# A two-layer gated block on one core: when the token combinations of the first feed-forward pass are made

## The reference, cut to what matters

```
x = x + tanh(g_xattn[0]) * linear_attention(layernorm(x), ctx, ctx)
x = x + tanh(g_ffn[0])   * ffn0(layernorm(x))        # weights stored as 4-bit codes
x = x + tanh(g_xattn[1]) * autocorrelation(layernorm(x), ctx, ctx)
x = x + tanh(g_ffn[1])   * ffn1(layernorm(x))

ffn0(x1):
    Wg, Wu, Wd = NF4[codes] * absmax per block of 64         # 1024 -> 2752 -> 1024
    y1 = x1 @ Wg + x1 @ g_lora_a @ g_lora_b
    y2 = x1 @ Wu + x1 @ u_lora_a @ u_lora_b
    x3 = relu(y1) * y2
    return x3 @ Wd + x3 @ d_lora_a @ d_lora_b
```

## Time and profile before

| | us |
|---|---|
| median of 3 runs | 2003.04 (2002.95 to 2003.74) |
| the profiled execution | 2003.48 |
| its span, first to last instruction | 2001.5 |
| first matmul of pass 0's products (start) | 187.65 |
| first matmul of pass 1 (start) | 346.25 |

### The profile page before, as it was taken

The page is one execution under the profiler, slowest core; times in us unless marked ns, Lnnn a source line. Parts: engine busy times, 40 slices in busy tenths (PEclk is TensorE's granted clock), DMA queues, the critical chain, the costliest instruction groups (busy, mean ns, idle before and its releaser), DMA issues. The chain is left out here.

```text
span 2001.5 us, 26467 instructions
## 1 busy us (share of the span) xinstructions
PE 1918.8 (96%) x9140; PEld 963.6 (48%) x9140; DVE 1293.8 (65%) x2204; ACT 1254.9 (63%) x1998; POOL 835.4 (42%) x752
## 2 busy tenths in 40 slices
PE   6996888999999999999999999999998899999998
PEld 5774334444444444444444445444444455555554
DVE  5776888364564736555473644636379988888872
ACT  6995668886777677676777776677524343443431
POOL 2443884222223223232232333222268667667742
PEclk9997998999999999999999999999999999999999
DMA  5651545856637375573737556373531110111001
GB/s 201 223 171 55 193 163 195 292 193 215 232 122 265 105 257 190 178 249 127 265 109 252 192 172 227 99 253 117 210 137 59 32 41 29 53 53 38 27 22 42
DMA packets 91989, 303.01 MB, mean 151 GB/s; under 512 B 11984, under 2 KB 16720, under 8 KB 73168
## 3 DMA queue, kind: packets, MB, share of 16 engines
q1 hardware_dynamic: 91856, 301.32, 44.3%
HBM read 274.01 MB, written 27.26 MB: 151 GB/s over the span
## 5 line engine op out<-in xcount | busy, mean ns | idle before, releaser
L1036 ACT ACTIVATE first<-first 128x512 f32<-128x512 int32 x1008 | 625.7, 626 | 27.4 <-DVE wt L1439 1.8
L1265 POOL TENSOR_TENSOR gu<-wt,gu 128x512 f16<-128x512 f32 x86 | 102.3, 1190 | 370.6 <-ACT gu L1055 370.5
L1439 DVE SCALAR_TENSOR_TENSOR wt<-first,w_scale,absm 128x512 f32<-128x512 f32 x132 | 102.6, 777 | 227.4 <-ACT first L1036 226.8
L1785 PE MATMUL a_psQ<-z,gu 128*128 128x512 f16 x936 | 208.5, 379 | 0.0
L2386 PE MATMUL a_psL<-z,l_x 128*128 128x512 f16 x768 | 170.7, 379 | 1.0 <-DVE l_x L2488 0.8
L1785 PE MATMUL a_psC<-z,gu 128*128 128x512 f16 x732 | 167.8, 379 | 0.0
L1785 PE MATMUL a_psC<-z 128*128 128x512 f16 x684 | 156.9, 379 | 0.0
L1785 PEld LDWEIGHTS a_psQ<-z,gu 128*128 128x128 f16 x936 | 91.5, 98 | 110.5
L1277 POOL TENSOR_TENSOR hid_lo<-z,hid_hi 128x512 f16<-128x512 f32 x76 | 90.2, 1201 | 118.7 <-ACT hid_hi L1096 118.6
L1265 POOL TENSOR_TENSOR dn_lo<-wt,dn_hi 128x512 f16<-128x512 f32 x42 | 50.3, 1197 | 199.2 <-ACT dn_hi L1055 199.2
L1442 DVE SCALAR_TENSOR_TENSOR wt<-a_psE,lora_gain,wt 128x512 f32<-128x512 f32 x132 | 99.1, 751 | 44.6 <-PE a_psE L1747 24.4
(11 more groups left out here) (418 smaller groups left out, 4122.3 us busy)
## 6 DMA issues: line engine op xcount, KB each, us to landing
z<-x_parts SPq DMA_DIRECT2D x140, 1024.0 KB, 5.8
first<-in_codes SPq DMA_DIRECT2D x132, 256.0 KB, 3.0
absm<-in_absmax SPq DMA_DIRECT2D x264, 128.0 KB, 3.3
X<-in_x SPq DMA_DIRECT2D x16, 512.0 KB, 4.3
c_in<-in_ctx SPq DMA_DIRECT2D x16, 512.0 KB, 5.3
cT<-in_ctxT SPq DMA_DIRECT2D x16, 512.0 KB, 3.6
o_sp<-in_w SPq DMA_DIRECT2D x16, 512.0 KB, 4.8
z<-in_ctx SPq DMA_DIRECT2D x8, 1024.0 KB, 7.0
```

The lines of the kernel that those rows point to most:

```text
L1036: act.activation(level[w % 2][:], codes[w % RING] if k == 0 else level[w % 2][:], ACT.Prelu, bias=bias, scale=scale, alpha=alpha).then_inc ...
L1265: pool.tensor_tensor(low, source, high, ALU.subtract).then_inc(wlo_done, 1)
L1439: dve.scalar_tensor_tensor(wt[at], source[:], w_scale[:, m:m + 1], absm[w % RING][:], ALU.mult, ALU.mult).then_inc(scaled, 1)
L1785: mm = pe.matmul(out, w[:, k * P:(k + 1) * P], xx[:, k], start=first and q == 0, stop=q == 3 * KD // 2 - 1, skip_group_check=True)
```

## The change

Two edits. `folding` spreads the sixteen parts otherwise: in the product steps they stand in steps 1, 2, 4, 5, 7, 8, 10, 11, 13 and 14, two of three, and the last six stand in steps 16 to 21, beside the downs. The last three slots of the ring are filled in step 22 instead of 20.

```diff
         def folding(s):


-            i, part = divmod(s - 1, 2)
-            return (i, part) if 0 <= i < B else None
+            order = [t for t in range(1, 16) if t % 3] + list(range(16, 22))
+            return divmod(order.index(s), 2) if s in order else None
...
                         for t in range(2):
                             load_x(t)
-                    if s == 20:
+                    if s == 22:
                         for c in range(2):
                             sp.wait_ge(prod_mm[c], 8)
                         wait_parts(4 * B)
```

## The result

The changed kernel takes 2019.84 us (median of 4 runs, 2018.89 to 2020.17). The kernel before, run beside it, takes 2003.39; the ratio is 1.0078, 95% interval 1.0061 to 1.0096. The forecast of 2007.3 had the sign right and the size wrong: 12.5 us too low, and outside its range. The profiled execution is 2020.17 with a span of 2018.2, 16.7 us longer than before.

What follows compares the result with a forecast made beforehand. PE, busy 96% of the span, was taken as the bound; 10.4 us gained ahead of pair 7 and 14.3 lost behind it, taken as +4.3, made 2003.48 into 2007.8, median 2007.3, range 1998.8 to 2012.

Steps and rivals of the forecast that it cites:

- the product steps: Pass 0 ahead of the downs: DVE's hidden values of pair 7 start at 293.5 instead of 303.87, 10.4 us earlier.
- Unit 7: PE's 6.9 us wait in pass 0 for POOL's low half of weight unit 7, forecast to fall to about 4.
- the 5 us before the downs: PE's wait for DVE's hidden values of pair 7: of 8.2 us some 5 remain.
- the wait for `lora_b`: PE's 3.0 us wait on DVE in pass 0, forecast to shrink to about 1.
- DVE is the later one beside the downs: In the down steps, 21 combination instructions ahead of accumulate 20 make DVE late: 14.3 us lost behind pair 7.
- the sum: DVE's durations from pair 7's hidden values to the last combination, 47.7 us; with the product steps, +4.3 in all.
- S: PE's first matmul of pass 1, at 346.25 before, forecast at 350.2; its shift is carried to the end one for one.
- The clock rival: Close waits in the downs keep PE at 1.2 GHz, the six last downs take 7.8 us more: 2015; chance 0.05.
- pair 7 to S: From the start of DVE's hidden values of pair 7 to S: 56.7 us instead of 42.4.
- the forecast's own sign: If right, DVE has no wait of over 2 us from pair 7's hidden values to S.
- The ring: Slots 2 to 4 issued at 351.0 instead of 329.55; slot 2, needed at 360.8, comes in time: costed at nothing.
- Behind S: In pass 1 the first product copies are done by S + 9.8, PE wants them at S + 10.6: no loss.

Runs made afterwards that it cites:

- e4_both: Changed kernel with ring slots 0 and 1 filled in step 15 and the second layer's factor loads moved ahead of slots 3 and 4; ratio 1.0026.
- e7: As e4_both, but DVE's combination instructions of sequences 5 to 7 work on 16 of 512 columns; ratio 0.9981.
- e3: Changed kernel with ring slots 0 and 1 filled in step 15 instead of 18; ratio 1.0068.
- e2: Changed kernel with the loads of the second layer's two factors moved to step 22, ahead of ring slots 3 and 4; ratio 1.0045.
- e1: Kernel before with only the ring's edit, slots 2 to 4 in step 22; 2007.97 us against 2004.79, ratio 1.0013.
- e8: As e4_both, but POOL's combination instructions of sequences 5 to 7 work on 16 of 512 columns; ratio 0.9970.
- e12: Kernel before with steps 3, 7, 11, 15 free of combinations, five parts beside the downs, slots 0-1 in step 15, 2-4 in step 21; 2013.6 us, ratio 1.0041.
- e5: Kernel before with step 14 free of combinations, two parts in steps 16 and 17, ring unchanged; 1999.12 us, ratio 0.9972.
- e6: Kernel before with steps 14 and 16 free of combinations, parts in 17 and 18, slots 0 and 1 in step 15; 1999.52 us, ratio 0.9971.
- e9: Kernel before with steps 3, 9, 14 free of combinations, four parts beside the downs, slots 0-1 in step 15, 2-4 in step 21; 2013.1 us, ratio 1.0047.
- e10: Kernel before with steps 3, 7, 10, 14 free of combinations, five parts beside the downs, slots 0-1 in step 15, 2-4 in step 21; 2006.8 us, ratio 1.0012.

## Why the prediction was wrong

**Right: the product steps.** Pair 0 to pair 7 is 82.1 (forecast 293.5 - 211.85 = 81.7). Unit 7 and the 5 us before the downs came as walked, and the wait for `lora_b`, forecast at 1, is gone.

**Right in kind: DVE is the later one beside the downs.** e4_both, which leaves this and little else, is at 1.0026: 5.2 us where the sum had 4.3. In both kernels the 21 combination instructions took 21.7 us (forecast 22.9; mean 1.03 instead of 1.09), and from the last of them to S are 8.95 us (forecast 9.0). The closeness is partly luck: in e4_both DVE's waits are 3.7 us more than summed, and the other terms 2.4 less. The clock rival did not come about in the changed kernel: the granted clock, down to 0.50 in 325 to 330, is 1.00 in the last downs.

**Mis-sized: the waits inside pair 7 to S.** The last combination ends 52.1 us behind pair 7, forecast 47.7. DVE waits for POOL's low halves 1.88, 2.15 and 1.40 us, where the sum had 1.7 for them, and 3.55 for ACT's decoding of unit 16, where it had 0.5. By the forecast's own sign (no wait of DVE of over 2 us) both 2.15 and 3.55 spoke against it. The first error is of size: the chain through POOL and ACT is longer than walked, and e7, with DVE's share almost empty, still takes 49.6. The second is a step that was not there: the sum gave SP's stores their usual landing and did not ask what stood ahead of them on the queue. e3, and e4 with it, take 2.9 us of that wait away and shorten pair 7 to S by 2.4 and 3.0.

**Failed: "The ring" and "Behind S".** The ring was costed at nothing because its own slots would come in time, which they did: PE did not wait at its third product (364.04). I looked at what the ring's loads need and who needs them, and not at what stands behind them on the same queue. "Behind S: No loss" compared the copies with PE's need by ACT's work alone; L1134, which stands between the copies of the first and the second product, waits for a transfer. It cost 7.8 us (28.97 - 21.16), and e2 shows it by taking it away whole. Put at nothing, this is the largest part of the miss. The profiled execution lies 12.4 us above the sum: 7.8 here, 4.3 in pair 7 to S (61.0 instead of 56.7), 1.7 in the second layer (below), and -1.4 for the rest, mostly an earlier start of pair 0. The row was to be had before: ACT already waited 2.44 us there, with 1.9 to spare for PE.

The Trainium skill (DMA: Bandwidth & Descriptors, Queues, rings and completion order) says that each DMA engine takes the descriptors of one queue's ring in ring order. By this a small load waits until the large ones ahead of it have been served, and the rows agree: 11.7 instead of 6.4 us behind three slots, 9.5 instead of about 3 behind two. How much a load loses is not set by the slots ahead of it alone: behind one slot the later factor takes 7.8 us in e2 and 9.1 in e4_both, and what makes this difference is not shown.

**The last piece, 1.7 us.** It is far from the change, in the second layer, and was in nobody's forecast. PE there waits 2.12 us for DVE in both kernels and then runs small matmuls. Before, then after:

```profile
1571.57 1.10 PE L2278 MATMUL a_psE<-made,z 128*128 128x512 f32 x2 [2.12 <-DVE n_x L2558]
1572.50 1.02 PE L2278 MATMUL a_psE<-z 128*128 128x512 f32 x2
...
1583.65 0.59 PE L2282 MATMUL a_psQ<-first,z 128*128 128x512 f16 x2 [0.66 <-DVE X L2564]
```

```profile
1586.59 1.35 PE L2278 MATMUL a_psE<-made,z 128*128 128x512 f32 x2 [2.12 <-DVE n_x L2558]
1587.73 1.92 PE L2278 MATMUL a_psE<-z 128*128 128x512 f32 x2
...
1600.36 0.81 PE L2282 MATMUL a_psQ<-first,z 128*128 128x512 f16 x3 [0.66 <-DVE X L2564]
```

The same work takes 12.08 and 13.77 us, and the granted clock is 1.00 in the one and 0.66 to 0.77 in the other over the first 5 us. The long form shows in the profiled executions of the changed kernel, e1, e3, e4, e7, e8 and e12, the short one in before, e2, e5, e6, e9 and e10. One execution of each was profiled. The form follows neither of the changes; the time at which the stretch starts differs by up to 22 us. With it the span's 16.7 is accounted for: an earlier start of pair 0 (-1.5), pair 0 to 7 (-10.0), pair 7 to S (+18.7), S to fourth (+7.8), and this (+1.7).

## What to carry to other kernels

When a bulk transfer is moved, price three things: whether it comes in time itself, what stands behind it on its queue, and which engine that runs in order waits for those small transfers, since what is queued behind such a wait is the real bill. An edit that is nearly free by itself (the ring's, 0.9 us behind S here) can cost many times that (7.8) beside another, because it has used up the slack that the other needs. (The new order without the ring's edit was not run.) And before work is moved beside another stage, count that stage's idle time from its window: DVE had 4 us free beside the downs, so one part more (with a gap ahead of the last pair) gave 0.28%, and five more cost 0.26% even with both meetings taken away.

## What I had not expected of the hardware

- A store of 256 KB behind two loads of 1 MB on the same queue takes 9.0 to 9.5 us to land, where such stores take about 3 otherwise.
- A wait of 2.12 us of PE, the same in both kernels, is followed by full clock in one and by a granted clock of 0.66 to 0.77 for some 5 us in the other, worth 1.7 us at a place that the change does not touch. Seven of the thirteen profiled kernels show it, and why is open.
- Making either engine's share of one chain almost empty (DVE's or POOL's) gave the same 8.4 us: in the one case DVE was full, in the other the chain through POOL and ACT held it up.
- A DVE instruction of 16 columns takes 0.17 us, and 1.07 to 1.15 when it meets a POOL instruction of 1.15.
